# First cross attention: keys cut as 128 + 26, remainders of four heads in one transpose, two units in one product step

## The reference

```python
x = x + _L0_xattn_ref(_layernorm(x), ctx_1024, Wq, bq, Wkv, bkv, Wo, bo)

def _L0_xattn_ref(X, encoder_out, Wq, bq, Wkv, bkv, Wo, bo):   # 16 heads of 64
    Q = (X @ Wq.T + bq).reshape(b, lq, h, d)                    # 2 x 1024 queries
    KV = (encoder_out @ Wkv.T + bkv).reshape(b, lk, h, 2 * d)   # 2 x 154 keys
    K, V = (KV[..., :d], KV[..., d:])
    scores = jnp.einsum('bqhd,bkhd->bhqk', Q, K) / d ** 0.5
    weights = jax.nn.softmax(scores, axis=-1)
    attn = jnp.einsum('bhqk,bkhd->bqhd', weights, V).reshape(b, lq, h * d)
    return attn @ Wo.T + bo
```

## Time and profile before

| | |
|---|---|
| time, median of 3 runs | 2231.63 us |
| span of the profiled execution, first to last instruction | 2231.4 us |
| TensorE (PE) busy | 2014.9 us, 90% |
| PE weight loads (PEld) busy | 1695.9 us |
| VectorE (DVE) busy | 1555.8 us, 70% |
| ScalarE (ACT) busy | 1249.7 us, 56% |
| GpSimd (POOL) busy | 907.4 us, 41% |
| mean granted TensorE clock | 0.942 |

### The profile page before, as it was taken

The page is one execution under the profiler, slowest core; times in us unless marked ns, Lnnn a source line. Parts: engine busy times, 40 slices in busy tenths (PEclk is TensorE's granted clock), DMA queues, the critical chain, the costliest instruction groups (busy, mean ns, idle before and its releaser), DMA issues.

```text
span 2231.4 us, 65049 instructions
## 1 busy us (share of the span) xinstructions
PE 2014.9 (90%) x26562; PEld 1695.9 (76%) x26562; DVE 1555.8 (70%) x4222; ACT 1249.7 (56%) x3476; POOL 907.4 (41%) x1053
## 2 busy tenths in 40 slices
PE   5799999999998999986899868898998889999997
PEld 4688888887885788875799747676666778888886
DVE  5876777677653566555577348786788769888886
ACT  3645545554512667761455447786885436666664
POOL 2443344334322444432488744452021004566654
PEclk9999999999999999998899979999997689999999
DMA  4101010100201200001255220000000017777764
GB/s 132 53 12 41 31 40 12 40 31 12 74 3 51 77 21 21 12 21 67 78 125 118 37 83 2 2 3 31 2 2 23 15 60 208 184 177 164 182 153 96
DMA packets 101456, 139.37 MB, mean 62 GB/s; under 512 B 33252, under 2 KB 79848, under 8 KB 99752
## 3 DMA queue, kind: packets, MB, share of 16 engines
q1 hardware_dynamic: 80040, 104.93, 15.1%
q0 software_dynamic: 21120, 30.29, 7.8%
HBM read 111.86 MB, written 23.33 MB: 61 GB/s over the span
## 4 chain that ended last, share of the span: by engine, by line
PE 46%; DVE 11%; issue 6%; POOL 4%; DMA 2%; ACT 2%; POOLq 0%; SPq 0%; DVEq 0%; ACTq 0%
PE bank L3243 8%; PE bank L2013 8%; PE bank L1600 4%; PE bank L1681 2%; PE bank L2436 2%; DVE f_Y L3427 2%; PE bank L2827 2%; PE bank L1665 2%; PE bank L1648 1%; PE bank L2423 1%; PE bank L2880 1%; PE bank L2850 1%; PE bank L2457 1%; PE bank L2864 1%; PE bank L2442 1%
## 5 line engine op out<-in xcount | busy, mean ns | idle before, releaser
L1111 DVE SCALAR_TENSOR_TENSOR a_acc<-a_praw,a_convw,a_acc 128x256 f32<-128x256 f32 x345 | 196.8, 577 | 9.5 <-ACT a_acc L1260 1.2
L3521 POOL DMA_INDIRECT out<-f_Y,f_id x78 | 132.2, 1695 | 140.7 <-DVE f_Y L3427 87.2
L1198 DVE COPY_PREDICATED wa<-masks,bank 128x512 f32<-128x512 uint8 x128 | 93.4, 732 | 94.6 <-PE bank L1012 94.4
L3243 PE MATMUL bank<-f_exT,f_wp 128*128 128x256 f32 (+1 forms) x816 | 148.8, 330 | 5.2 <-DVE f_wp L611 2.7
L911 PE MATMUL bank<-XT,wa 128*128 128x256 f32 x512 | 146.3, 415 | 0.0
L3243 PEld LDWEIGHTS bank<-f_exT,f_wp 128*128 128x128 f32 x816 | 121.9, 191 | 19.8 <-DVE f_Hp L3408 3.5
L309 POOL TENSOR_SCALAR rs<-mv 128x2 f32<-128x2 f32 x42 | 11.9, 283 | 307.2 <-DVE mv L290 306.7
L1826 POOL TENSOR_TENSOR b_P<-b_P,b_rec 128x616 f32<-128x616 f32 x64 | 77.6, 1213 | 116.9 <-DVE b_rec L1735 116.9
L1336 ACT ACTIVATE wa<-bank 128x256 f32<-128x256 f32 x160 | 59.1, 384 | 109.1 <-PE bank L998 108.2
L998 PE MATMUL bank<-wa 64*64 64x64 f32 x2560 | 104.6, 225 | 13.6 <-DVE wa L1198 6.9
L2610 ACT ACTIVATE d_P<-d_P,d_mx 128x256 f32<-128x256 f32 (+1 forms) x256 | 106.8, 484 | 14.8 <-DVE d_mx L2537 12.6
(11 more groups left out here) (493 smaller groups left out, 6094.4 us busy)
## 6 DMA issues: line engine op xcount, KB each, us to landing
wa<-in_f_w SPq DMA_DIRECT2D x114, 384.0 KB
wa<-in_c_w SPq DMA_DIRECT2D x64, 256.0 KB, 3.2
wb<-grown SPq DMA_DIRECT2D x4, 1536.0 KB, 7.8
a_KQg<-grown SPq DMA_DIRECT2D x4, 1536.0 KB, 7.4
a_E<-decays SPq DMA_DIRECT2D x16, 256.0 KB, 3.8
X<-in_x SPq DMA_DIRECT2D x4, 512.0 KB, 5.4
wa<-in_a_wqkv SPq DMA_DIRECT2D x1, 2048.0 KB, 8.6
summed<-X SPq DMA_DIRECT2D x8, 256.0 KB, 2.1
```

Of the source, the lines that this page charges most:

```text
L1111: i = v.e.scalar_tensor_tensor(A_, praw[:, c, :, j:j + BT_], convw[:, c, j:j + 1], A_, ALU.mult, ALU.add)
L1198: i = v.e.copy_predicated(xx[c % 2], masks[:, l].unsqueeze(2).broadcast_to([P, 2, H, R]), b.ap.rearrange("p (w h r) -> p w h r", w=2, h=H))
L3243: i = t.e.matmul(out_, lhsT[x], rhs[y], start=n == 0 and first, stop=n == 2 and last_, skip_group_check=True)
L3521: g.e.indirect_dma_start(out_rows, bass.IndirectOffsetOnAxis(ido[t % 4][:, m:m + 1], 0), Y[t % 2][:, m, :], None, bounds_check=B * T - 1, ...
```

## The change

The number of keys stays 154, but the cut is now 128 + 26 (`REST = 26`). Of each head the first 128 keys are transposed by themselves (4 per unit), and the last 26 keys of all four heads of the unit, gathered in a buffer `Pr` of 128 x 4 x 32 (`SLOT = 32`, the six columns after each 26 cleared once), by one transpose. With two row halves each this makes 10 transposes of 64 x 128 instead of 16 of 64 x 77. Their output is 128 x 320 per bank instead of 77 x 512.

- The values of the first 128 keys are computed as before (`V`, four products instead of eight). The remainders' values, `VR`, are computed by `rest`, two entries in rounds 4 and 5: 2 contraction parts x 4 matmuls of 128 x 26 by 256 columns, one in each 32-column slot of the array. VectorE adds the bias in four operations each. `VR` is cleared first, and holds for each group of four heads two blocks of 64 partitions: slots 0 and 1 (one pair) and slots 2 and 3, each head's values in its own 64 columns.
- `mix` now takes two units together, in even steps only, two banks. Per pair of units: 4 matmuls of the remainders (64 x 128 by 128) and 8 matmuls over 128 keys (128 x 64 by 128); before, 16 matmuls over 77 keys. ScalarE and VectorE still take out 128 x 256 twice per pair of units.
- GpSimd scales in two operations: 128 x 104 into `Pr`, 128 x 512 in place. It also clears `Pr` and `VR` at the start of the stage (five memsets).
- `PT` is a ring of four instead of two.

```diff
-                order += [("value", i // 4, i // 2 % 2, i % 2)] + ...
+                order += [("value", i // 2, i % 2)] * (i < 4) + [("rest", i - 4)] * (4 <= i < 6) + ...
...
-                order += [("mix", u - 3)] * (0 <= u - 3 < U)
+                order += [("mix", (u - 4) // 2)] * (u % 2 == 0 and 0 <= u - 4 < U)
...
+                    elif what == "rest":
+                        first = s[1] * S2 + P
+                        free(t, *s)
+                        for j in range(KD):
+                            for g in range(4):
+                                i = t.e.matmul(b.ap[slot(g), 0:4 * XD], ctxT[:, j, first:first + REST], by_quad(wv[:, j, :])[:, :, g, :],
+                                               start=j == 0, stop=j == KD - 1, tile_position=(0, g * SLOT),
+                                               skip_group_check=True)
...
+                        t.wait_ge(cleared, 2)
...
+                        for i in range(5):
+                            for half, rows_ in enumerate(halves):
+                                b = at[s + (half,)]
+                                part = Pm[u % NPB][rows_, i // 2, i % 2, 0:P] if i < 4 else Pr[u % NPB][rows_, :, :].rearrange("p g n -> p (g n)")
+                                y = t.e.transpose(by_slot(b.ap)[:, i, :], part, ident[rows_, rows_],
+                                                  tile_position=(rows_.start, 0))
...
+                        for i, u, q in pair_:
+                            for j in range(2):
+                                t.e.matmul(at[s + (j,)].ap[:, cols(i)], VR[halves[j], bb, q, :], PT[u % NPB][halves[j], 4, :],
+                                           start=i == 0, stop=False, tile_position=(halves[j].start, 0), skip_group_check=True)
+                        for j in range(2):
+                            for i, u, q in pair_:
+                                for par in range(2):
+                                    y = t.e.matmul(at[s + (j,)].ap[rows(par), cols(i)], V[:, bb, 4 * q + 2 * j + par, :],
+                                                   PT[u % NPB][:, 2 * j + par, :], start=False, stop=True,
+                                                   tile_position=(0, par * XD), skip_group_check=True)
...
-                        v.e.tensor_copy(PT[u % 2][:, :, :, :, halves[0]], by_head(b.ap)).then_inc(b.emptied, 1)
+                        v.e.tensor_copy(PT[u % NPB][:, :, halves[0]], by_slot(b.ap)).then_inc(b.emptied, 1)
...
+                for i in range(NPB):
+                    y = g.e.memset(Pr[i][:, :, REST:SLOT], 0.0)
+                y.then_inc(cleared, 1)
+                g.e.memset(VR[:, :, :, :], 0.0).then_inc(cleared, 1)
...
-                        g.e.tensor_tensor(p_, p_, bc(rec[:, u % NPB].rearrange("p a b -> p (a b)"), S2),
-                                          ALU.mult).then_inc(scaled.sem, 1)
+                        r_ = rec[:, u % NPB].rearrange("p a b -> p (a b)")
+                        g.e.tensor_tensor(Pr[u % NPB][:, :, 0:REST], p_[:, :, P:S2], bc(r_, REST), ALU.mult)
+                        g.e.tensor_tensor(p_[:, :, 0:P], p_[:, :, 0:P], bc(r_, P), ALU.mult).then_inc(scaled.sem, 1)
```

More of the change, by code:

```diff
@@ L24 @@
 HALF = S2 // 2
+REST = S2 - P
+SLOT = 32
 EPS = 1e-5
@@ L1547, in stage_b @@
                     continue
+                elif what == "mix":
+                    for j in range(2):
+                        at[s + (j,)] = banks[4 + turns % 4]
+                        at[s + (j,)].turn(*k, j)
+                        out_high.mark(s[1], j)
+                        turns += 1
+                    continue
                 else:
@@ L1657, in tensor @@
                         t.wait_ge(scaled.sem, scaled.at[u,])
+                        t.wait_ge(cleared, 2)
                         for half in range(2):
                             free(t, *s, half)
-                        for par in range(2):
-                            for j in range(2):
[L1662 to L1677, removed]
@@ new lines, in tensor @@
+                        for i in range(5):
[4 more added lines that the diff above has]
+                                                  tile_position=(rows_.start, 0))
+                                if i == 4:
+                                    y.then_inc(b.filled, 1)
+                    elif what == "mix":
+                        p = s[1]
+                        bb = p // 2 // TB
+                        pair_ = [(i, 2 * p + i, (2 * p + i) % 4) for i in range(2)]
+                        cols = lambda i: slice(i * P, (i + 1) * P)
+                        for i, u, q in pair_:
+                            emptied(t, "turn", u, 0)
+                            emptied(t, "turn", u, 1)
+                        emptied(t, "value", 1, 1)
+                        emptied(t, "rest", 1)
+                        for j in range(2):
+                            free(t, *s, j)
+                        for i, u, q in pair_:
+                            for j in range(2):
+                                t.e.matmul(at[s + (j,)].ap[:, cols(i)], VR[halves[j], bb, q, :], PT[u % NPB][halves[j], 4, :],
+                                           start=i == 0, stop=False, tile_position=(halves[j].start, 0), skip_group_check=True)
@@ L1794, in scalar @@
                             for j in range(2):
-                                i = c.e.activation(Pm[u % NPB][:, par, j, :], pair(half.ap)[:, j, :], ACT.Exp,
-                                                   bias=mx[:, u % NPB, par, j:j + 1], accum_out=total[:, u % NPB, par, j:j + 1])
+                                i = c.e.activation(Pm[u % NPB][:, j, par, :], pair(half.ap)[:, j, :], ACT.Exp,
+                                                   bias=mx[:, u % NPB, j, par:par + 1], accum_out=total[:, u % NPB, j, par:par + 1])
                             i.then_inc(half.emptied, 1)
```

86 lines of the change are left out of this document (49 added, 37 removed).

## The result

| | before | after |
|---|---|---|
| median, us | 2232.32 (2229.62 to 2237.86, 4 runs) | 2213.75 (2210.14 to 2218.72, 4 runs) |
| span of the profiled execution, us | 2231.4 | 2209.6 |

The ratio is 0.9911, with a 95% interval of 0.9885 to 0.9938: 18.6 us at the medians, 21.8 between the two profiled spans. 2212 or 2213 was forecast.

A forecast was written before the change was run, and what follows sets the result against it. PE was taken as the bound, busy 90% of the span, with the loop through VectorE and POOL only 0.1 us behind. Before the periods -5.5, six periods -7.2, after them -6.2: -18.9 us, so 2212 or 2213; range 2199 to 2226.

The forecast's parts named there:

- transposes to the next group: PE's ten transposes per unit: 0.45 us instead of 0.64 to the next group, bounds 0.40 to 0.66.
- products of a pair: PE's products with the values for two units: 1.57 us instead of 2.04, bounds 1.45 to 1.65.
- even to odd, odd to even: Plain steps, transposes to transposes: 3.55 and 3.15 us, together 6.70 where two steps took 6.38.
- m = 4 to 5, 5 to 6: Two steps a period with statistics and norms: 4.47 us becomes 4.71, and 3.70 becomes 3.62.
- first value product to T2: Stage start up to step 2's transposes: 4.9 us less on PE, 0.24 more for the first scale.
- T53 to T65: Late steps behind the six periods, mostly units without queries: 5.5 us less, including 1.5 in a half-clock stretch.
- from T65 on: Stage end: 24 records instead of 32 after the last transposes, at half clock, less an uncovered copy: 0.7 us less.
- rival 3: Transposes go by weight columns, so their group stays at 0.66 us: 12 us less gained, 2224; chance 0.06.
- The loop: Transposes, VectorE copy, reciprocal, POOL scale, next transposes: no step is shorter; 2.84 us after, 2.99 before, 3.78 when maxima bind.
- 1 (PE bounds throughout, 2199): PE stays the bound because POOL's two operations cost no more than one: all 27 and 4.9 us come off; chance 0.12.
- 2 (POOL's second operation dear): POOL's split scale costs 0.6 us more instead of 0.24, 10 us over the loop-bound steps: 2223; chance 0.17.
- 4 (the clock falls in every period): PE's waits at m = 5 halve its clock for 5 us, costing 2.4 to 5 each; at 4, 2240; chance 0.09.

The follow-up runs named there:

- experiment 2: Changed kernel with the products of one unit in every step, into two banks, instead of pairs in even steps; 2226.21 us, ratio 0.9950 to the kernel before.
- experiment 4: Kernel before, its tiles kept, with products of two units together in even steps and four PT buffers; 2235.10 us, ratio 1.0002 to the kernel before.
- experiment 6: Kernel before with reciprocal and scale moved ahead of maxima and copy, exponentials a step earlier, behind the copy; 2241.10 us, ratio 1.0011 to the kernel before.
- experiment 5: Changed kernel with reciprocal and scale moved ahead of maxima and copy, exponentials a step earlier, behind the copy; 2223.36 us, ratio 0.9927 to the kernel before.
- experiment 10: Changed kernel with exponentials a step earlier, between products and query, and VectorE's reciprocal between maxima and copy; 2220.57 us, ratio 0.9956 to the kernel before.
- experiment 9: Changed kernel with VectorE's reciprocal moved ahead of the copy, behind the maxima, nothing else; 2209.02 us, ratio 0.9897 to the kernel before.

## Why the prediction was right

The time, the sign and the mechanism of the periods came as forecast. Some terms were off in both directions, and that the sum fits so well is partly luck, as the part on the end shows.

| step | forecast | measured | |
|---|---|---|---|
| transposes to the next group | 0.45 | 0.40 (odd), 0.30 (even) | |
| products of a pair | 1.57 | 1.62 | 0.60 + 1.02 |
| VectorE copy | 0.49 | 0.484 | |
| POOL, 104 and 512 columns | 1.45 | 0.368 + 1.049 | |
| plain odd step, scores to next transposes | 3.78 | 3.87 | exponentials level with the copy |
| even to odd, odd to even | 3.55, 3.15 | 3.46, 3.24 | the sum is 6.70 in both |
| output step | 4.81 | 4.66 to 4.76 | |
| m = 4 to 5, 5 to 6 | 4.71, 3.62 | 4.63, 3.78 | |
| period | 31.75 | 31.56 | |
| first value product to T2 | -4.65 | -3.5 | |
| T2 to T5 | -0.8 | -0.7 | |
| six periods | -7.2 | -8.3 | |
| T53 to T65 | -5.5 | -6.6 | |
| from T65 on | -0.7 | -3.6 | the clock before |
| sum | -18.9 | -22.7 | in the profiles |

*Transposes.* Ten records of 128 weight columns (1280 in all) hold PE for 0.40 us until the queries and 0.30 until the products, where sixteen of 77 (1232 in all) held it for 0.64 until the products. The count decides, at about 0.04 each, and rival 3 is out. The Trainium skill (TensorE: Matmul & The Clock Gate, LDWEIGHTS) says that the load's time scales with the columns; by it the group would have stayed as it was, and for this shape the trace disagrees. So 0.45 was 0.05 too much; the forecast's own lower bound, by count, was right.

*Products.* 1.62 is 0.05 above the forecast and inside its bounds. The two errors cancel: transposes and products together are 1.92 in the even step, 2.02 forecast. The Trainium skill (TensorEngine Tiling (Array Packing), Key Properties) says that a change of tiling mode drains the array. The products over 128 keys take 1.02 behind the remainders' as they took 1.02 behind the transposes, so if there is such a cost, it doesn't grow here.

*The loop and the two kinds of step.* This was the step that carried the forecast, and it is shown. Taking away POOL's 104 columns shortens exactly the odd-to-even step and m = 4 to 5, by what POOL saves (experiment 3). Moving the same products to the other steps, where they meet the output projection, costs 1.6% (experiment 1). The two factors, crossed, give the period:

| us | products singly | in pairs, even steps |
|---|---|---|
| tiles of 77 keys | 32.95 | 34.00 |
| tiles of 128 + 26 | 32.74 | 31.56 |

The pairs gain nothing by themselves: with the old tiles an even step holds PE for 4.06 to 4.13, too much for the 3.09 that the odd step gives back. With the new tiles the even step (3.46 to 3.51) stays near the loop, and the output projection fills the odd steps. That the tiles gain nothing by themselves is not shown, since experiment 2 brought in the wait for a bank, 1.7 a period, which is more than the 1.2 that lies between it and the change. Over the stage the change is 9.0 us shorter than experiment 2, and that one 13.7 shorter than the kernel before, of which the start is 3.5 and the tail 4.8.

*The start.* Here a term was mis-sized. The remainder products cost 1.00 each, as priced. But the stretch of four value products (now two remainder products) and five queries up to the first scores went from 10.52 us to 6.74, 3.8 less and not 4.9. Two things took the rest. A query behind a long value product took 0.71; now the one behind the first remainder product takes 0.91 (731.36 to 732.27) and the last one, behind a wait, 0.90; the lengthening comes to 0.4 in all. That a long product covered a gap at a group's first weight load is argued. And the last query waits for a bank: VectorE adds the remainders' bias in two groups of four operations (1.72 us each), and PE stands 0.69 for the second, a wait that the forecast had at nothing. To T2 3.5 are left.

*The end.* Forecast -6.2, measured -10.2: the largest miss, and in the kernel's favour. It has two parts.

From T53 to T65 the forecast's terms come to -5.5, and 6.6 came off. The clock doesn't make this difference. The loss by it, 5 us times (1 - clock) summed over windows, is 3.4 us in this stretch before (the earlier trace rows and the row below, from 980 us) and 3.4 after (955 to 980 us, above).
```profile
990.00:995.00 5.00, 4.53 (x69) 3.96 (x69) 3.04 (x8) 4.19 (x20) 1.21 (x1) 0.84 0.01 2
```
Most of the excess is the first of these steps, m = 5 to 6: it went from 3.70 to 2.84, and the forecast had given it the 0.1 of the other periods.

From T65 on, 0.7 was forecast and 3.6 came off, and here it is the clock of the kernel before. These are its last products, and those of experiment 4, the same records at full clock:
```profile
1002.79 3.68 PE L1681 MATMUL bank<-b_PT,b_V 77*64 77x128 f32 x32
```
```profile
1007.11 1.97 PE L1681 MATMUL bank<-b_PT,b_V 77*64 77x128 f32 x32
```
That is 1.7; the transposes ahead of them take 1.14 against 0.70, and the 24 output matmuls 4.81 against 2.68 from first to last. Together it is 4.3, the whole difference of the two tails (16.02 and 11.72). The forecast had TensorE at half clock there after the change too. But its work there ran at full clock (1.00 from 980 to 990 us), and the clock fell only where PE waited 5.56 us for the layer norm. Put beside experiment 4's tail, the change's (12.43) is 0.7 longer, not 0.7 shorter.

So 4.3 of the 22.7 hang on the clock in the one profile of the kernel before. How often it meets that isn't known: in experiment 6, its own work in another order, the last windows have 0.80 and 0.84, in experiment 4 1.00. No run isolates it. Without them 18.4 are left, near the medians' 18.6 and the forecast's 18.9, but that is luck in part: errors of +1.2 at the start, +0.1 behind it, -1.1 in the periods, -1.1 in the late steps and +1.4 in the tail cancel.

*Rivals.* 1 (PE bounds throughout, 2199): PE waits 15.9 us for POOL in the stage. 2 (POOL's second operation dear): 1.42 for the two, below the 1.45 of the forecast. 4 (the clock falls in every period): it stays 1.00 from 750 to 955 us, and the least busy window there, from 785 to 790 us, has 3.61 of 5. Only behind the periods does it fall, to 0.67 from 960 to 965, after a window busy 3.42. The forecast's reason against it, that the waiting comes in two parts, fits; it wasn't tested by itself. The mechanism is real, as experiments 1, 5 and 10 met it. A fall cost 1.5 to 2.0 us there, less than the 2.4 to 5 that the forecast took.

*What stays open.* Whether experiment 9's order beats the change (ratios 0.9897 and 0.9911, with overlapping intervals); whether the new tiles with single products in one bank each would do as well; and why opening the loop lengthened the steps at m = 5 to 7, of which only the waits named in experiment 5 and the falls of the clock were seen.

## What to carry to other kernels

Find, for every kind of step in a period, which comes last, the engine's own work or the loop through the others; work taken from one engine is worth its time only in the steps that this engine bounds. Moving work between steps can be worth more than removing it, and a move that gains nothing by itself may gain together with a removal, so test them crossed; then look in each run of the cross for a wait that only it has, as the bank in experiment 2. A step that waits for a loop through two engines has more than one path in it: taking the nearest off (the copy here) moves nothing when another ends 0.01 us earlier.

## What the runs showed of the hardware

- GpSimd's scale with a broadcast factor: 128 x 104 in 0.37 us, 128 x 512 in 1.05, 128 x 616 in 1.21. Splitting it cost 0.2.
- Sixteen records of 26 weight columns by 256, in four column slots, last 1.07 us, 1.00 to the next group; the 32 records by 128 of stage D have as many columns, and last 1.08. A value product, 4 records of 77 weight columns by 512 without column slots, takes 1.72 for half as many columns, so the slots overlap at this width too.
- Six query matmuls take 0.71 us behind a value product or behind other queries, and 0.90 to 0.91 behind a remainder product or the products with the values.
- What PE did before the clock fell to 0.66 in a stretch of five microseconds: it was busy 3.24 of the five before (experiment 1), 3.25 and in another period 3.73 (experiment 5), 3.38 and in another period 3.82 (experiment 10). In the change it was busy 3.61 and 3.82 in the like places and kept 1.00, and in experiment 1 it was busy 3.24 a period earlier and kept it too. So the busy time of such windows alone doesn't tell the cases apart.
- The same 32 records of products (77 x 128) last 3.68 us where the granted clock is 0.68 and 0.50 in the windows from 1000 to 1010 us (kernel before), and 1.97 where it is 1.00 (experiment 4).
